# Feed-forward part of a sandwich block: the down products trail by one half step more

## The reference

```python
x = x + _layernorm(_L0_attn_ref(_layernorm(x, axis=-1), ...), axis=-1)
x = x + _layernorm(_L0_ffn_ref(_layernorm(x, axis=-1), ...), axis=-1)
```

```python
gate_out = x_flat @ gate_w.T          # gate_w = gate_t * gate_s[:, None], 1792 x 512
up_out = x_flat @ up_w.T              # up_w the same with up_t, up_s
hidden = jax.nn.silu(gate_out) * up_out
out_flat = hidden @ down_w.T          # down_w = down_t * down_s[:, None], 512 x 1792
```

## Time and profile before

| what | us |
|---|---|
| median of 3 runs | 2463.42 |
| lowest and highest | 2460.84, 2470.95 |
| the profiled execution | 2465.49 |
| its span, first to last instruction | 2463.7 |
| PE busy | 2364.7 (96%) |
| POOL, DVE, ACT busy | 1684.8, 1399.0, 1190.3 |

### The profile page before, as it was taken

How to read it: one execution, slowest core, us unless ns; L and a number is a source line. 1 busy time by engine, 2 the same in 40 slices (tenths; PEclk the granted TensorE clock), 3 DMA queues, 4 the chain that set the end, 5 groups by cost and what they waited for, 6 DMA issues and landing times.

```text
span 2463.7 us, 38243 instructions
## 1 busy us (share of the span) xinstructions
PE 2364.7 (96%) x12256; PEld 2014.4 (82%) x12256; DVE 1399.0 (57%) x2479; ACT 1190.3 (48%) x1719; POOL 1684.8 (68%) x1331
## 2 busy tenths in 40 slices
PE   4799999999999999999999999999999999999996
PEld 3588888888888888878888888888888887777775
DVE  5456666666666566656555555555555555544635
ACT  6544444444444444435554445554444444555553
POOL 4577777777777777756777777777777774564564
PEclk7899999999999999999999999999999999999998
DMA  3634444444343443464444444443333335221222
GB/s 107 209 120 124 124 127 128 128 122 126 124 125 126 126 123 121 126 226 147 140 134 130 135 128 127 131 136 118 109 112 114 115 115 193 104 68 60 69 72 83
DMA packets 156936, 304.94 MB, mean 124 GB/s; under 512 B 22464, under 2 KB 88000, under 8 KB 154176
## 3 DMA queue, kind: packets, MB, share of 16 engines
q1 hardware_dynamic: 143856, 279.37, 36.1%
q10 hardware_dynamic: 13008, 24.65, 2.9%
HBM read 216.92 MB, written 87.03 MB: 123 GB/s over the span
## 4 chain that ended last, share of the span: by engine, by line
PE 89%; POOL 3%; DVE 2%; DMA 2%; issue 2%; ACT 1%; SPq 0%; DVEq 0%; POOLq 0%; ACTq 0%
PE proj L1936 55%; PE yp L1936 18%; PE sc L2002 4%; PE sc L1979 4%; PE sc L2005 4%; PE sc L1992 4%; DMA v_tok<-v_blocks 1%; DMA nw<-norm_w 0%; DVE stats L1335 0%; DMA fs_stage<-ffn_scales 0%; ACT y L831 0%; DMA y<-x 0%; POOL stage L675 0%; POOL w_odd L586 0%; DMA x_blocks<-stage 0%
## 5 line engine op out<-in xcount | busy, mean ns | idle before, releaser
L1936 PE MATMUL proj<-xb,w_odd 128*128 128x512 f32 x2688 | 709.3, 402 | 17.9 <-POOL w_odd L579 13.0
L1936 PE MATMUL proj<-xb,w_even 128*128 128x512 f32 x2688 | 683.0, 397 | 16.4 <-DMA xb<-x_blocks 3.8
L1936 PEld LDWEIGHTS proj<-xb,w_even 128*128 128x128 f32 x2688 | 499.8, 190 | 118.6 <-issue 8.3
L1936 PEld LDWEIGHTS proj<-xb,w_odd 128*128 128x128 f32 x2688 | 492.7, 190 | 113.1 <-POOL w_odd L579 13.9
L601 POOL TENSOR_TENSOR qd<-q,table 128x512 f32<-128x512 f32 x128 | 164.6, 1299 | 221.9 <-ACT q L947 221.9
L1524 DVE TENSOR_TENSOR g<-sc,g 128x512 f32<-128x512 f32 x128 | 88.5, 691 | 272.3 <-ACT sq L961 272.3
L592 POOL TENSOR_TENSOR ow_lo<-v_tok,ow_hi 128x1024 fp32r<-128x1024 f32 x32 | 76.4, 2388 | 234.0 <-ACT ow_hi L915 234.0
L1531 DVE TENSOR_TENSOR y<-yp,y 128x512 f32<-128x512 f32 x240 | 164.6, 686 | 103.6 <-PE yp L1936 102.0
L1936 PE MATMUL proj<-x_t,f_hi 128*128 128x512 f32 x896 | 215.6, 393 | 2.8 <-issue 2.8
L1936 PE MATMUL yp<-ow_hi,g_hi 128*128 128x512 f32 x512 | 202.5, 395 | 1.3 <-DVE y L1531 1.3
L1936 PEld LDWEIGHTS proj<-x_t,f_hi 128*128 128x128 f32 x896 | 170.5, 191 | 39.1 <-issue 2.9
(11 more groups left out here) (169 smaller groups left out, 4352.0 us busy)
## 6 DMA issues: line engine op xcount, KB each, us to landing
raw<-w_attn SPq DMA_DIRECT2D x128, 512.0 KB, 3.7
k_blocks<-pd SPq DMA_DIRECT2D x64, 512.0 KB, 3.7
k_tok<-k_blocks SPq DMA_DIRECT2D x256, 128.0 KB, 3.0
v_blocks<-vf SPq DMA_DIRECT2D x64, 512.0 KB, 2.7
v_tok<-v_blocks SPq DMA_DIRECT2D x256, 128.0 KB, 3.0
v_tok<-w_out SPq DMA_DIRECT2D x32, 512.0 KB, 4.4
fraw<-w_ints SPq DMA_DIRECT2D x13, 1024.0 KB, 4.9
tile_a<-w_ints ACTq DMA_DIRECT2D x42, 256.0 KB, 3.5
```

Of the source, the lines that this page charges most:

```text
L1936: last = pe.matmul(psum, s, m, start=start and n == 0, stop=n == len(terms) - 1, skip_group_check=more)
```

## The change

PE runs in the first half of step m the tiles 2 and 3 of `down(m - 2)`, and in the second half the tiles 0 and 1 of `down(m - 1)`. DVE's additions follow in the same order. `down_split_hi` is cut in two: the conversion of `draw` (`down_convert`) stays at the start of the odd step, and the rounding to `d_hi` goes to the head of the second half. On POOL `down_split_lo` goes there too. Ahead of step 3, PE runs two tiles of `down(1)` and no longer four; behind step 27 it runs six tiles and no longer four of `down(27)` with two of `down(26)` inside the step.

```diff
@@ -726,9 +726,9 @@
                                    ALU.subtract).then_inc(hlo_done, 1)
 
             def hidden(m, par, split=None, down=None):
-                if down is not None:
-                    down_split_lo(down)
                 for t in range(2):
+                    if down is not None and t == 1:
+                        down_split_lo(down)
                     hidden_lo(m, par, t)
                     if split is not None:
                         ffn_split_lo(split, t)
@@ -1216,10 +1216,12 @@
                     act.activation(x_t1[:, s - 2, 0, t].rearrange("p h n -> p (h n)"), sc[t % 2][:, :],
                                    ACT.Copy).then_inc(xhi_done, 1)
 
-            def down_split_hi(n, d):
+            def down_convert(n):
                 act.wait_ge(draw_in, 16 * (n + 1))
                 act.activation(draw[:, :, :].bitcast(F32), draw[:, :, :], ACT.Copy)\
                     .then_inc(dcv_done, 1)
+
+            def down_split_hi(n, d):
                 act.wait_ge(dcv_done, n + 1)
                 wait(act, down_done, 4 * d)
                 act.activation(d_hi[:, :, :], draw[:, :, :].bitcast(F32), ACT.Copy)\
@@ -1246,8 +1248,10 @@
                 if scales is not None:
                     act.wait_ge(fs_ready, scales + 1)
                 if down is not None:
-                    down_split_hi(down, m - 1)
+                    down_convert(down)
                 for t in range(2):
+                    if down is not None and t == 1:
+                        down_split_hi(down, m - 1)
                     ffn_silu(m, t)
                     if split is not None:
                         ffn_split_hi(split, t, m)
@@ -1279,6 +1283,7 @@
             gated_hi(last, 0, 1)
             ffn_convert(1)
             ffn_silu(1, 0)
+            down_convert(0)
             down_split_hi(0, 0)
             hidden_hi(1, 1, 0)
             ffn_split_hi(1, 0, 1)
@@ -1811,21 +1816,21 @@
                         dve.wait_ge(ln_own, own[0])
                     tile_statistics(lambda t: y2_tile(s, t), norm_c[s], t)
 
-            def ffn_step(m, d, seg, scales=None, first=False, turn=None):
+            def ffn_step(m, segs, scales=None, first=(False, False), turn=None):
                 if scales is not None:
                     new_scales(scales)
                 for t in range(2):
                     hidden(m, t)
                     if turn is not None:
                         mid_lo(turn, (2 * t, 2 * t + 1))
-                    add_down(d, seg, 2 * t, first)
-                    add_down(d, seg, 2 * t + 1, first)
+                    for u in range(2):
+                        add_down(m - 2 + t, segs[t], 2 - 2 * t + u, first[t])
 
             def numbered_step(m, turn=None):
 
-                d = m - 1
-                ffn_step(m, d, 2 * (d // (2 * FG)) + d % 2, scales=m // 2 if m % 2 == 0 else None,
-                         first=d % (2 * FG) < 2, turn=turn)
+                ffn_step(m, [2 * (d // (2 * FG)) + d % 2 for d in (m - 2, m - 1)],
+                         scales=m // 2 if m % 2 == 0 else None,
+                         first=[d % (2 * FG) < 2 for d in (m - 2, m - 1)], turn=turn)
 
             last = STEPS - 1
             new_scales(0)
@@ -1853,7 +1858,7 @@
             rms(1, sc[0])
             variances_a(2)
             variances_a(3)
-            for t in range(CH):
+            for t in range(2):
                 add_down(1, 1, t, first=True)
             numbered_step(3)
             norm_scales(norm_a[2])
@@ -1890,12 +1895,9 @@
             norm_scales(norm_c[1])
             with dve.Fori(FG + 4, ROUNDS - 1) as n:
                 for j in range(2):
-                    ffn_step(2 * n + j, 2 * n + j - 1, 2 + (j + 1) % 2, scales=n if j == 0 else None)
+                    ffn_step(2 * n + j, (2 + j, 3 - j), scales=n if j == 0 else None)
             numbered_step(FSTEPS - 2)
-            hidden(FSTEPS - 1, 0)
-            for t in range(2):
-                add_down(FSTEPS - 2, 2, t)
-            hidden(FSTEPS - 1, 1)
+            numbered_step(FSTEPS - 1)
             for t in range(2, CH):
                 add_down(FSTEPS - 2, 2, t)
             for t in range(2):
@@ -2241,7 +2243,10 @@
                         units(m, t, seg)
                         if turn is not None:
                             mid_transposes(turn, (2 * t, 2 * t + 1))
-                        down(m - 1, (2 * t, 2 * t + 1))
+                        if t == 0:
+                            down(m - 2, (2, 3))
+                        else:
+                            down(m - 1, (0, 1))
 
                 pe.wait_ge(x_t_in[0], 16 * 2)
                 units(0, 0, 0)
@@ -2265,7 +2270,7 @@
                 project_out(last, CH + 2, downs=CH)
                 project_out(last, CH + 3, downs=CH)
                 sums_of_squares(1, sc[0])
-                down(1, outs=BT)
+                down(1, (0, 1), outs=BT)
                 for m in range(3, 2 * FG):
                     ffn_step(m, m % 2, {10: 2, 12: 3}.get(m))
                 for m in range(2 * FG, 2 * FG + 8):
@@ -2278,10 +2283,13 @@
                             for u in range(2):
                                 ffn_unit(narrow, 2 * n + j, 2 + j, 2 * t + u, n if j == 0 else None)
                             for u in range(2):
-                                project_down(narrow, 2 * n + j - 1, 1 - j, 2 * t + u,
-                                             n if j == 1 else None)
+                                if t == 0:
+                                    project_down(narrow, 2 * n + j - 2, j, 2 + u)
+                                else:
+                                    project_down(narrow, 2 * n + j - 1, 1 - j, u, n if j == 1 else None)
                 ffn_step(FSTEPS - 2, 2)
                 ffn_step(FSTEPS - 1, 3)
+                down(FSTEPS - 2, (2, 3))
                 down(FSTEPS - 1)
 
             with pe.If(needs_lo == 1):

```

## The result

The changed kernel took **2443.83 us** (median of 5 runs, 2442.45 to 2445.4) against 2463.42 for the kernel before (5 runs beside it, 2460.84 to 2471.99): ratio 0.9914, 95% interval 0.99 to 0.9928, so 0.9% faster. Forecast were 2441.5 with a range of 2436 to 2451. In a second comparison it took 2441.12 (6 runs) against 2464.01 (11 runs), ratio 0.9911 [0.9891, 0.993]. The profiled execution of the first took 2444.16 (span 2442.4), 21.3 us less than that of before.

The account below looks back on a forecast made before the run. TensorE, busy 96% of the span, was taken as the bound, so only its stops and slow matmuls could be won. 23.4 - 3.2 + 1.7 = 21.9 us off the profiled 2465.5 gave 2443.6, as median 2441.5, range 2436 to 2451.

Parts of the forecast that it names:

- The cause and the five stops: PE stops in steps 5, 9, 11, 19 and 21, 12.67 us, waiting for ACT's late `d_hi`; 23.4 us lost with slow matmuls.
- Step 5's margin: In step 5 `d_hi` would be done at 2170.2, due at 2170.9: 0.7 us to spare, where it was 2.8 late.
- Rival A: The 0.7 us margin isn't there; steps 5, 9 and 11 keep stops, 9 us come back: 2450 us, chance 0.17.
- The kept loss of 3.2 us: Of the 23.4 us lost on PE, 3.2 would remain, as short stops and restarts in steps 19 and 21.
- Step 19: ACT enters this step 1.2 to 1.7 us later against 0.7 of margin; a PE stop of 0.5 to 1.0 stays.
- Step 21: Lateness handed on by `last_residual` and the late start leaves a PE stop of 1.0 to 1.6 us here.
- DVE starts `hid` at T + 5.9 because of the statistics: In step 17, 5.9 us after its start on PE; `h_hi` then ends at 7.3 and `fraw` lands 1.2 us late.
- only some 4 us ahead of it: On the DMA side, `draw`'s load now precedes `fraw`'s by about this; half the bytes, it should be through by then.
- The ends: Ahead of step 3, 2.1 us gained; behind step 27, 0.3 to 0.5 lost; net gain 1.7 us.
- Rival B, the ring: `fraw` conversion, POOL's run and load in series, 19.8 us against 21.8 a round; slower from 23.9, up to 2488; chance 0.04.
- The sum: Over the whole kernel, 23.4 us lost less 3.2 kept plus 1.7 at the ends: 21.9 us gained.

Follow-up runs that it names:

- `d_lo` last: The changed kernel with `d_lo` on POOL moved behind both `f_lo`, at the end of the odd step: 2469.96 us, ratio 1.0014 to the kernel before.
- the exchange alone: The changed kernel with only SP's order changed, `fraw`'s load for round n + 1 ahead of `draw`'s for round n: 2442.3 us, ratio 0.9918.

## Why the prediction was right, step by step

**The cause and the five stops: right.** All was put on ACT being late with `d_hi` for what is queued ahead of it. Moving only the normalisations brought 18.9 us; moving only the product on PE left no wait for `d_hi`. The granted clock is 1.00, as said.

**Step 5's margin: right.** 0.7 us were forecast. ACT's timeline there, which answers the earlier trace rows:

```profile
2162.44 2.92 ACT L831 ACTIVATE y<-y,shift,rstd 128x512 f32<-128x512 f32 x4
...
2168.30 1.04 ACT L1227 ACTIVATE d_hi<-draw 128x1024 fp32r<-128x1024 f32 x1
```

`d_hi` ends at 2169.34 and the pair starts at 2170.15 in the chain (its first matmul at 2169.99), 0.65 to 0.8 later. Rival A fell with it.

**The kept loss of 3.2 us: about right in sum, wrong in its places.** What is left is 276.04 - 273.67 = 2.4. Only about 1.2 of it stand where the 3.2 were put, in steps 19 and 21; another 1.0 stand in a step that was not named, so part of the agreement is luck. PE's two stops in the stretch are the ones of the chain above, both for `d_hi`: 0.73 in step 9 and 0.78 in step 21.

- *Step 19* was to keep 0.5 to 1.0 and kept 0.13. The step that failed is "DVE starts `hid` at T + 5.9 because of the statistics" in step 17. In the trace of after DVE's rows are

```profile
2300.26 0.17 DVE L1351 TENSOR_SCALAR var_eps<-meanvar 128x4 f32<-128x4 f32 x1
2300.34 0.75 DVE L1792 SCALAR_TENSOR_TENSOR hid<-proj,fs,hid 128x512 f32<-128x512 f32 x1
```

with T at 2296.2, so it starts at T + 4.1. Before, the same small instruction took 1.93 us:

```profile
2315.97 1.93 DVE L1346 TENSOR_SCALAR var_eps<-meanvar 128x4 f32<-128x4 f32 x1
```

POOL's `d_lo` (2315.47 to 2317.87) ran beside it then; the change itself has moved `d_lo` away. I had seen that row inside T + 5.9 and not asked what made it long. POOL's run began at T + 6.25 and not T + 7.3, and took 10.5; the load landed 0.57 after ACT was free.
- *Step 21* was to keep 1.0 to 1.6 and kept 0.78, with a slow restart of 0.27: the lateness that step 19 was to hand on was smaller.
- *Step 9* was not named and kept 0.73, with 0.25. Its load of `fraw` took 6.65 and not 4.9, a term of 1 us that the sum lacked. The prediction had looked at this load for one danger, `draw`'s load "only some 4 us ahead of it", and held that `draw` "should be through by then". It was: `draw` went out 3.58 us ahead and landed after 3.5, and in eight other rounds with the same distance `fraw` took 4.8 to 5.1. By the Trainium skill (DMA: Bandwidth & Descriptors, "Issuing engines are not separate DMA queues") transfers run on the same 16 engines and interleave; the trace agrees where two loads do overlap, 7.30 us for the 1 MB with `draw` 0.86 ahead (`d_lo` last) against 4.9 alone, but that is not the case here. What stood beside step 9's load is one packet of 16 KB on a queue that the DMA view calls `instruction`. The DMA view of three windows that follow each other (2198.8 to 2203.5, to 2204.45, to 2204.7) has one queue in each (packets, MB, share):

```profile
q1 hardware_dynamic: 278, 1.05, 67.5%
...
q8 instruction: 1, 0.02, 6.3%
...
q1 hardware_dynamic: 10, 0.00, 5.4%
```

278 of the 288 packets (of `fraw` and of the small load of scales behind it) had started when it came; the last ten started only after it. The second profile of the change has the same picture and 6.64. Such a packet also stands beside loads of 5.0 (the one of 2335.83), so its mere presence costs nothing. It is the likely cause, by its place in front of the last packets; no run moved it, so it is not shown.

**The ends: right.** 2.1 ahead and 0.4 back were forecast; measured 2.2 and 0.5.

**Rival B, the ring: not in the change, but near.** As written it has a round of 19.8 us against 21.8. The trace of after has less room than that: in the six rounds in which ACT waited, 21.85 to 22.7 us lie between one conversion of `fraw` and the next, since the ring holds more than its sum in some rounds: normalisations, POOL instructions that take longer beside DVE's (`h_lo` 1.74, `f_lo` 2.85), step 9's slow load. ACT's slack took these waits in all steps but 9 and 21 and, by 0.13 us, 19. The run with `d_lo` last shows that its price was sound (23.9 us a round is no gain) and that one more thing was missing in it: the ring also runs through SP's queue. An edit of four lines on POOL that looks like a gain of 2.4 us closes it.

**The sum.** Forecast 21.9 us, measured 22.7 in the three lengths: the stretch 21.0 (forecast 23.4 - 3.2 = 20.2), the ends 1.7 (forecast 1.7). By these lengths the medians should be 2463.4 - 22.7 = 2440.7 and, in the second comparison, 2464.0 - 22.7 = 2441.3. Measured are 2443.83 and 2441.12: the second is what the lengths say, the first 3.1 above it, of which the profiled execution has 1.4 in the part ahead. What remains open is why the end of that unchanged part moves by up to 6 us from profile to profile; no run here was made for it.

## What to carry to other kernels

When a tensor engine near 100% stops in a few odd places, follow what it waits for to the queue of the engine that makes it, and move either the product later or the work ahead of it in that queue; each did most of it here. Before giving an engine a new order, write down every ring (buffer, its last reader, the queue that reloads it, the load, its first reader) with its sum against the round, the queue of the DMA issuer included: the same change with `d_lo` two places later lost all it had won. And ask of a long row in the old trace what ran beside it, since the change may move just that.

## What the runs showed of the hardware

- A small DVE instruction beside POOL: `var_eps` (128x4) took 0.17 us alone and 1.93 beside a `TENSOR_TENSOR` of POOL, more than a 128x512 one (0.69). It ended at 2317.90, just behind POOL's `d_lo` (2317.87). By the Trainium skill (SBUF — State Buffer, "Who interferes with whom") copies and `tensor_scalar` can take the ports that they share with GpSimd, and then one waits for the whole of the other. The trace agrees: what counts is POOL's instruction (2.40), not the size of DVE's.
- Two loads that overlap: 1 MB took 4.9 to 5.0 us in the kernel before, where the 512 KB had long landed, and 6.4 to 7.9 (median 7.4) with 512 KB issued 0.9 to 1.4 us ahead. Issued first (the exchange alone), the big one had 5.1 at most and the 512 KB took 5.1 to 6.5. With the 512 KB 3.6 us ahead and just landed, as in the change, the 1 MB took 4.8 to 5.1, but for step 9's.
- The clock, a mix of the 1.2 and the 2.4 GHz level: it fell behind all five stops of PE of 4.7 to 4.9 us (0.74 in four, 0.87 in one, from the start of the stop) and behind the three of 3.8 to 4.3 in the run with `d_lo` last; behind those of 2.5 to 3.0 it fell in nine and stayed at 1.00 in three; behind 1.5 and less it was 1.00 each time in the stretch. The matmuls behind a stop of 4.73 cost some 3 us more (3.75 + 4.61 against 1.81 + 3.63), and those behind the first stop of before, of only 2.78, as much (3.75 + 4.79).
